# Folded query and key weights, a first group in halves, and a zero fill by DMA in a two-layer attention kernel

## The reference

```python
# first block
h = film(rmsnorm(x, norm1_w), cond, film1_w, film1_b)
Q = h @ q_w + q_b; K = h @ k_w + k_b; V = h @ v_w + v_b
attn = softmax(einsum('bnd,bmd->bnm', Q, K) * D ** (-0.5))
x = x + (einsum('bnm,bmd->bnd', attn, V) @ proj_w + proj_b)
h = film(rmsnorm(x, norm2_w), cond, film2_w, film2_b)
x = x + gelu(h @ mlp_w1 + mlp_b1) @ mlp_w2 + mlp_b2
# second block: mod = silu(c) @ ada_w.T + ada_b, in six parts
h = layernorm(x) * (1 + scale_msa) + shift_msa
x = x + gate_msa * attention(h, padding_mask)      # 16 heads of 8
h = layernorm(x) * (1 + scale_mlp) + shift_mlp
x = x + gate_mlp * (gelu_tanh(h @ fc1_w.T + fc1_b) @ fc2_w.T + fc2_b)
```

## Time and profile before

| | us |
|---|---|
| median of 3 runs | 182.25 |
| lowest and highest | 182.13, 182.42 |
| the profiled execution | 182.43 |
| its span, first to last instruction | 180.7 |
| busy: PE, PE weight load | 172.1, 133.9 |
| busy: DVE, ACT, POOL | 116.0, 107.7, 107.5 |

### The profile page before, as it was taken

The page is one execution under the profiler, slowest core; times in us unless marked ns, Lnnn a source line. Parts: engine busy times, 40 slices in busy tenths (PEclk is TensorE's granted clock), DMA queues, the critical chain, the costliest instruction groups (busy, mean ns, idle before and its releaser), DMA issues.

```text
span 180.7 us, 5691 instructions
## 1 busy us (share of the span) xinstructions
PE 172.1 (95%) x2250; PEld 133.9 (74%) x2250; DVE 116.0 (64%) x349; ACT 107.7 (60%) x274; POOL 107.5 (59%) x176
## 2 busy tenths in 40 slices
PE   6988999999999999989999999999899999999994
PEld 6965888587485798767678876888788765668594
DVE  0694569978106069867756878768688556696333
ACT  2338858871993651667576766767877596623500
POOL 5499979899910905995005333359979877690000
PEclk9999999999999999999999999999999999999999
DMA  4999999702247200300110001100000000001103
GB/s 111 341 425 429 424 421 426 337 13 39 51 175 308 102 0 4 120 7 3 62 39 32 2 5 64 64 2 5 5 7 7 5 0 5 0 0 58 62 0 116
DMA packets 5334, 19.31 MB, mean 107 GB/s; under 512 B 572, under 2 KB 1292, under 8 KB 3980
## 3 DMA queue, kind: packets, MB, share of 16 engines
q1 hardware_dynamic: 4988, 18.27, 26.2%
q10 hardware_dynamic: 320, 0.68, 1.2%
HBM read 7.24 MB, written 1.09 MB: 46 GB/s over the span
## 4 chain that ended last, share of the span: by engine, by line
PE 47%; POOL 26%; issue 17%; DVE 6%; DMA 3%; ACT 0%; POOLq 0%; ACTq 0%
PE ps L328 8%; PE ps L337 7%; PE ps L315 6%; PE ps L307 6%; PE ps L265 4%; POOL gtmp L1222 4%; POOL xb L1224 4%; POOL xc L1217 3%; POOL xn L1252 3%; POOL rstd L1143 3%; PE ps L239 3%; POOL xs L1231 3%; DMA xs<-x 3%; POOL gated L1228 3%; PE ps L270 2%
## 5 line engine op out<-in xcount | busy, mean ns | idle before, releaser
L1028 DVE TENSOR_REDUCE nm<-ps 128x4 f32<-128x512 f32 x64 | 42.1, 683 | 17.1 <-PE ps L380 16.6
L765 ACT ACTIVATE shared<-ps 128x512 f32<-128x512 f32 x64 | 34.5, 596 | 18.8 <-PE ps L380 18.8
L380 PEld LDWEIGHTS ps<-k_pad,q_pad 32*128 32x128 f32 x512 | 29.7, 186 | 9.7 <-issue 5.9
L380 PE MATMUL ps<-k_pad,q_pad 32*128 32x128 f32 x512 | 35.0, 282 | 1.7 <-DVE nm L1028 1.3
L380 PE MATMUL ps<-q_pad,k_pad 32*128 32x128 f32 x512 | 35.0, 283 | 0.0
L380 PEld LDWEIGHTS ps<-q_pad,k_pad 32*128 32x128 f32 x512 | 29.3, 186 | 0.4 <-issue 0.2
L1143 POOL TENSOR_TENSOR rstd<-var_eps,half 128x4 f32<-128x4 f32 x16 | 16.4, 1025 | 20.9 <-DVE var_eps L886 15.2
L1228 POOL TENSOR_TENSOR gated<-attn,gate 128x128 f32<-128x128 f32 x16 | 7.3, 459 | 27.2 <-ACT attn L784 27.2
L446 PE MATMUL ps<-shared,vx 128*32 128x128 f32 x512 | 17.3, 275 | 0.3
L813 ACT ACTIVATE hid<-ps,W 128x512 f32<-128x512 f32 x16 | 10.9, 688 | 9.7 <-PE ps L328 9.7
L446 PEld LDWEIGHTS ps<-shared,vx 128*32 128x32 f32 x512 | 13.1, 109 | 3.0 <-issue 1.5
(11 more groups left out here) (135 smaller groups left out, 330.6 us busy)
## 6 DMA issues: line engine op xcount, KB each, us to landing
q_pad<-hid SPq DMA_DIRECT2D x1, 4096.0 KB, 21.9
k_pad<-hid SPq DMA_DIRECT2D x1, 4096.0 KB, 30.9
gate<-gates SPq DMA_DIRECT2D x1, 2048.0 KB, 6.6
xs<-x SPq DMA_DIRECT2D x4, 256.0 KB, 6.6
gate<-mask SPq DMA_DIRECT2D x1, 1024.0 KB, 11.8
q_pad<-apT SPq DMA_DIRECT2D x4, 256.0 KB, 2.4
k_pad<-apT SPq DMA_DIRECT2D x4, 256.0 KB, 2.4
W<-weights SPq DMA_DIRECT2D x1, 768.0 KB, 9.9
```

The lines of the kernel that those rows point to most:

```text
L380: return mm(bank(to)[:, t], held[some, t, b], moved[some, t, b], start=True, stop=True, skip_group_check=True)
L765: a(pT[b % 2][:, r], bank(of), ACT.Exp, scale=HD ** -0.5).then_inc(s["c_exp"], 1)
L1028: v.tensor_reduce(nm[b % 2][:, 4 * r:4 * r + 4], bank(of), AX.X, ALU.max, negate=True).then_inc(s["c_max"], 1)
```

## The change

Scores are computed as h (s q_w k_w^T) h^T with s = 1/sqrt(128): the 128x128 matrix and three bias terms are computed once on the chip, by four products ahead of the first transposes, and copied by ACT with the scale. One product per group then gives the query side, and the normalised input itself is the key side. The bias term that depends on the row rides as column 129 of the value product, and the exponentials' bias is made from the negated maximum by two small DVE operations. ACT now copies the query, and copies the value in two instructions.

In group 0, statistics of tiles 0 and 1 are DVE's, of 2 and 3 ACT's (Square with a sum); POOL normalises tiles 0 and 2, DVE 1 and 3; transposes signal in halves, and DVE applies scale and shift to tiles 0 and 1 and ACT to 2 and 3; the query product runs in two halves. Of group 1, ACT normalises two of the four tiles. The rows (384 KB) go from ACT's queue to SP's, the first layer's attention weights (256 KB) from SP's to ACT's. The zeros come from the upper half of `gate` rather than from hid[1], and the two vx tiles are zeroed by two DMAs on SP behind those of q_pad and k_pad, under the same semaphore; POOL's memsets of vx go, and its ones are written later. The diff, cut to what matters:

```diff
-_W = [("cond", B), ("film1", 2 * C), ("film2", 2 * C), ("cols0", 16), ("q", C), ("k", C), ("vt", C),
+_W = [("cond", B), ("film1", 2 * C), ("film2", 2 * C), ("cols0", 16), ("qt", C), ("kt", C), ("vt", C),
...
+        flat = shared.rearrange("p a g n -> p (a g n)")
+        v0 = [flat[:, 1024 + 520 * u:1024 + 520 * u + 516].rearrange("p (g c) -> p g c", g=G) for u in range(2)]
+        folded = flat[:, 2064:2064 + 2 * C + 3]
+        wvp, key_row, key_mat, query_key, query_bias = (folded[:, a:b] for a, b in (
+            (0, C + 1), (C, C + 1), (C + 1, 2 * C + 1), (2 * C + 1, 2 * C + 2), (2 * C + 2, 2 * C + 3)))
...
@@ sync (SP)
             for g in range(2):
                 sp.dma_start(xs[:, G * g:G * g + G], x[:, G * g:G * g + G]).then_inc(s[f"x_in{g}"], 16)
-            for n, (a, b) in enumerate((("q", "x_end"), ("ada", "q1"), ("mlp1", "m_end"), ("q1", None))):
+            sp.dma_start(R[:, :], rows.partition_broadcast(128)).then_inc(s["rows_in"], 16)
+            for g in range(2, 4):
+                sp.dma_start(xs[:, G * g:G * g + G], x[:, G * g:G * g + G]).then_inc(s[f"x_in{g}"], 16)
+            for n, (a, b) in enumerate((("ada", "q1"), ("mlp1", "m_end"), ("q1", None))):
...
-            zeros = hid[1][:].rearrange("p f b n -> p (f b n)")
+            zeros = gate[:, B // 2:B].rearrange("n b g c -> n (b g c)")
             sp.wait_ge(s["zero_ok"], 1)
             for to in (q_pad, k_pad):
                 sp.dma_start(to[:].rearrange("p t b n -> p t (b n)"), zeros.unsqueeze(1).broadcast_to((128, 4, B * N)))\
                     .then_inc(s["pad_zero"], 16)
-            sp.wait_ge(s["pad_zero"], 32)
+            for to in vx:
+                sp.dma_start(to[:].rearrange("n b z -> n (b z)"), zeros).then_inc(s["pad_zero"], 16)
+
+            sp.wait_ge(s["pad_zero"], 64)
             sp.wait_ge(s["aug_ok"], 3)
...
@@ tensor (PE)
             def a_first_norm():
                 for j in range(G):
+                    pe.wait_ge(s[("a_xn", "a_xd")[j % 2]], j // 2 + 1)
                     ins = nc.tensor.transpose(bank(0 if j < 2 else 4)[:, j], xn[0][:, j], ident[:])
+                    if j % 2:
+                        ins.then_inc(s[("a_TA", "a_T")[j // 2]], 1)
+
+            def a_first_query():
+                pe.wait_ge(s["fold_ok"], 1)
+                for half in range(2):
+                    pe.wait_ge(s[("a_hd", "a_h")[half]], 1)
+                    ins = mm(ps[:, 1, 2 * N * half:2 * N * half + 2 * N], key_mat, hT[0][:, 2 * half:2 * half + 2],
+                             start=True, stop=True, skip_group_check=True)
+                ins.then_inc(s["a_Q"], 1)
...
-                mm(ps[:, 1 + n, :], w("qk"[n]), hT[g % 2][:], start=True, stop=True).then_inc(s[("a_Q", "a_K")[n]], 1)
+            def a_query(g):
+
+                pe.wait_ge(s["a_h"], g + 1)
+                pe.wait_ge(s["a_qT"], g)
+                mm(ps[:, 1, :], key_mat, hT[g % 2][:], start=True, stop=True).then_inc(s["a_Q"], 1)
...
                 for j in range(G):
-                    ins = mm(bank(3)[:, j], hT[g % 2][:, j], wvp[:], start=True, stop=True, skip_group_check=True)
+                    to = ps[:, 3, 129 * j:129 * j + 129] if j < 3 else ps[:, 2, 0:129]
+                    ins = mm(to, hT[g % 2][:, j], wvp, start=True, stop=True, skip_group_check=True)
...
-                    ins = mm(bank(4 + 3 * u)[:, j], qT[u][:, j], kT[u][:, j], start=True, stop=True, skip_group_check=True)
+                    ins = mm(bank(4 + 3 * u)[:, j], qT[u][:, j], hT[u][:, j], start=True, stop=True, skip_group_check=True)
...
             warm(6)
+            pe.wait_ge(s["w_attn0"], 16)
+            pe.wait_ge(s["qcol_ok"], 1)
+            at = 2 * N
+            for lhs, rhs, size in ((w("qt"), col("cols0", COL["k_b"]), 1), (w("qt"), w("kt"), C),
+                                   (w("kt"), col("cols0", COL["q_b"]), 1), (qcol[:], col("cols0", COL["k_b"]), 1)):
+                ins = mm(ps[:, 6, at:at + size], lhs, rhs, start=True, stop=True, skip_group_check=True)
+                at += size
+            ins.then_inc(s["fold_mm"], 1)
             a_first_norm()
...
+            a_first_query()
+            pe.wait_ge(s["a_xa"], 1)
+            a_norm(1)
             a_value(0)
-            a_norm(1)
             a_scores(0)
             for g in range(3):
-                a_qk(g + 1, 0)
-                a_qk(g + 1, 1)
+                a_query(g + 1)
                 a_value(g + 1)
...
@@ scalar (ACT)
-            act.dma_start(R[:, :], rows.partition_broadcast(128)).then_inc(s["rows_in"], 16)
+            act.dma_start(W[:, W_AT["qt"]:W_AT["x_end"]], weights[:, W_AT["qt"]:W_AT["x_end"]]).then_inc(s["w_attn0"], 16)
...
+            act.wait_ge(s["x_in0"], 16)
+            for j in range(2, G):
+                a(gtmp[:, j], xs[:, j], ACT.Square, accum_out=first_sum[:, j - 2:j - 1]).then_inc(s["a_sq0"], 1)
...
-            def a_kv(g):
-                act.wait_ge(s["a_K"], g + 1)
-                a(kT[g % 2][:], bank(2), ACT.Identity, bias=col("cols0", COL["k_b"])).then_inc(s["a_kT"], 1)
+            def a_q(g):
+                act.wait_ge(s["a_Q"], g + 1)
+                a(qT[g % 2], bank(1), ACT.Identity, bias=query_key).then_inc(s["a_qT"], 1)
+
+            def a_v(g):
                 act.wait_ge(s["a_V"], g + 1)
-                a(v0[g % 2][:], bank(3), ACT.Copy).then_inc(s["a_v"], 1)
+                a(v0[g % 2][:, 0:3], ps[:, 3, 0:387].rearrange("n (b c) -> n b c", b=3), ACT.Copy)
+                a(v0[g % 2][:, 3], ps[:, 2, 0:129], ACT.Copy).then_inc(s["a_v"], 1)
...
+            a(folded[:, C:2 * C + 3], ps[:, 6, 2 * N:3 * N + 3], ACT.Copy, scale=C ** -0.5).then_inc(s["fold_ok"], 1)
+            act.wait_ge(s["film_ok"], 1)
+            affine("a_", 0, 0, bank(4), range(2, G))
             act.wait_ge(s["wvp_mm"], 1)
...
+            for j in range(2, G):
+                ins = a(xn[1][:, j], xs[:, G + j], ACT.Copy, scale=rstd[:, 0, G + j:G + j + 1])
+            ins.then_inc(s["a_xa"], 1)
+            a_q(0)
             affine("a_", 1, 0, bank(0))
+            a_v(0)
             a_exp(0)
...
-            act.wait_ge(s["pad_zero"], 32)
             b_gelus(1, range(2))
...
@@ vector (DVE)
+            for j in range(2):
+                v.bn_stats(bn[:, j], xs[:, j]).then_inc(s["a_first"], 1)
...
             def a_max(g):
                 u = g % 2
                 dve.wait_ge(s["a_S"], g + 1)
                 v.tensor_reduce(amax[:, u, :], bank(4 + 3 * u), AX.X, ALU.max, negate=True).then_inc(s["a_max"], 1)
+                dve.wait_ge(s["a_max"], g + 1)
+                dve.wait_ge(s["a_v"], g + 1)
+                row_term = v0[u][:, :, C]
+                v.scalar_tensor_tensor(out=amax[:, u, :], in0=amax[:, u, :], scalar=query_bias, in1=row_term,
+                                       op0=ALU.subtract, op1=ALU.subtract).then_inc(s["a_true"], 1)
+                dve.wait_ge(s["a_true"], 2 * g + 1)
+                v.scalar_tensor_tensor(out=emax[:, u, :], in0=amax[:, u, :], scalar=query_bias, in1=row_term,
+                                       op0=ALU.add, op1=ALU.add).then_inc(s["a_true"], 1)
...
@@ gpsimd (POOL)
-            p.memset(hid[1][:].rearrange("p f b n -> p (f b n)"), 0.0).then_inc(s["zero_ok"], 1)
+            p.memset(gate[:, B // 2:B].rearrange("n b g c -> n (b g c)"), 0.0).then_inc(s["zero_ok"], 1)
...
+                if k == 0 and g == 0:
+                    pool.wait_ge(s["a_sq0"], 2)
+                    p.tensor_scalar(var_eps[:, 0, 2:G], first_sum[:], 1.0 / C, EPS, ALU.mult, ALU.add).then_inc(s["a_ms0"], 1)
...
+            p.tensor_scalar(qcol[:], ident[:], 0.0, col("cols0", COL["q_b"]), ALU.mult, ALU.add).then_inc(s["qcol_ok"], 1)
             p.tensor_scalar(bcol[:], ident[:], 0.0, col("cols0", COL["v_b"]), ALU.mult, ALU.add).then_inc(s["bcol_ok"], 1)
...
-            for u in range(2):
-                p.memset(vx[u][:].rearrange("n b z -> n (b z)"), 0.0).then_inc(s["c_vinit"], 1)
...
             norm(1, 3, "b_")
             next_bias(3)
+            pool.wait_ge(s["pad_zero"], 64)
+            for t in vx:
...
```

More of the change, by code:

```diff
@@ L82, in build @@
         arden = sb("arden", [N, 2, G])
-        wvp = sb("wvp", [C, C])
+        qcol = sb("qcol", [C, N])
+        emax = sb("emax", [N, 2, G])
         bias_a = sb("bias_a", [N, C])
@@ L161, in stats_end @@
             n = G * k + g
-            return PER_GROUP * (n if n else 1)
+            return PER_GROUP * (n - 1)
         K_BANK = (7, 6, 6, 6)
@@ L690, in a_exp @@
             def a_exp(g):
                 u = g % 2
[L692 removed]
+                act.wait_ge(s["a_true"], 2 * g + 2)
                 for j in range(G):
[L694 removed]
+                    a(p0[u][:, j], bank(4 + 3 * u)[:, j], ACT.Exp, bias=emax[:, u, j:j + 1],
                       accum_out=aden[:, u, j:j + 1]).then_inc(s["a_exp"], 1)
             act.wait_ge(s["x_in1"], 16)
+            act.wait_ge(s["a_sq0"], 2)
@@ L698, in _ @@
             for j in range(G):
```

(39 more changed lines are left out.)

92 lines of the change are left out of this document (38 added, 54 removed).

## The result

The changed kernel takes 186.0 us (median of 4 runs, 185.49 to 186.41), the kernel before 182.33 on the same chip: a ratio of 1.0183 (95% interval 1.0135 to 1.0231). The forecast was 184.5 with 183.2 to 187.0 around it. The direction held and the size was within the range, but the wait that I had named is not in the profile.

What follows compares the result with a forecast made beforehand. PE was taken as the bound. Fills delay the spreads to 63.9, PE arrives 1.2 us sooner at 60.4 and waits, +2.3 us: 182.43 + 2.3 - 0.2 = 184.5 us, range 183.2 to 187.0.

Steps and rivals of the forecast that it cites:

- the wait that I had named: Before whole_scores(0): PE arrives at 60.4 and stands 3.5 us for both spreads, to 63.9; end moves by +2.3 us.
- The bound: Whole kernel: PE is busy nearly throughout; whatever delays PE at one point delays the end by as much.
- The term that decided the sum: Second layer: two vx fills on SP's queue add 4.88 us, so spreads land at 63.9 behind the gate read; +2.3 us.
- the first exponential starts at 15.6, where it started before: First layer, group 0: ACT's value copy ends at 15.1, DVE's corrections wait for it, exponentials start unchanged at 15.6.
- PE enters the MLP 1.2 us sooner: End of first layer: the folding's saving, taken as 1.2 us between bounds of 0 and 3.4.
- two small dependent operations ... 0.6 us in all: First layer, DVE behind each maximum: two added operations, priced from one of 0.16 us plus similar waits, 0.6 us.
- Rival (c): First layer not shortened at all; same 184.5 while PE comes by 63.9, 2.3 us later; 0.62 together with the main case.
- likewise if PE's wait is elsewhere: Sign against the forecast: it is wrong if PE waits somewhere other than for a spread before the first L380 group.
- the main case: Fills delay the spreads, PE waits before whole_scores(0): 184.5 us, own range 183.8 to 185.2; 0.62 together with rival (c).
- Rival (a): Clock falls in PE's 3.5 us stand for the spreads, costing 2.4 us more: 186.9; chance 0.16.
- Rival (b): Spreads not held behind the gate read, so the front's gain is kept: 181.0; chance 0.16 whole, 0.03 partly.
- The signs named in advance: Aug_rows near 42.3, gate read near 56.3, spreads right behind, PE idle 3 to 4 us, MLP entered near 31.

Runs made afterwards that it cites:

- the maximum first: Changed kernel with DVE taking group 0's maximum and two corrections ahead of group 3's statistics, fills left in: 187.99 us (187.16 to 188.74).
- the old queues: Changed kernel with group 0's maximum ahead, vx zeroed by POOL, and rows and attention weights back on their previous queues: 183.38 us, ratio 0.9998.
- both edits: Changed kernel with group 0's maximum ahead of group 3's statistics and vx zeroed by POOL again: 183.21 us median of ten runs, ratio 1.0.

## Why the prediction was right, and where it was not

- **The bound** held: PE's time to whole_scores(0) went into the end whole. 2.88 us late there, 3.06 us in the profiled execution (185.49 against 182.43).
- **The term that decided the sum**, the fills, was right as a mechanism and a little small: SP was put back by 5.65 us, not 4.88, the landings behind took 1.89 and 0.44 us less than before, so that the gate read moved by only 3.1 us where I had 4.88; but with the spreads behind it, it took 8.3 us and not 6.6, and in the profile of the fills alone PE stood until 64.4, not 63.9. That the landing came so near the forecast is partly two errors of opposite sign. The fills alone give 185.8 against 182.3, 3.5 us with 2.3 forecast; the profiled run has 2.8, and the two runs that lie highest are those with a clock of 0.991.
- **The step that failed** is the first layer: "the first exponential starts at 15.6, where it started before", and from it "PE enters the MLP 1.2 us sooner". The exponential came at 19.63, and PE entered 2.88 later. Three profiles split this. With the maximum first and a quick start, PE enters at 30.53, 1.55 us sooner than before. The slow start costs 2.02 (32.55). DVE's order costs another 2.41 (34.96, with the same slow start). So 2.88 = 2.02 + 2.41 - 1.55.
- In DVE's part, two terms were wrong. That the statistics of group 3 stand ahead of the first maximum is not in the forecast, so it was put at nothing: the maximum started at 17.32 and not 16.18, 1.14 us. And "two small dependent operations ... 0.6 us in all" was priced by a row in which POOL was not in the way: in group 0 they took 1.56 us, since the first stood beside POOL's addition, 1.30 us instead of 0.22. Moving the maximum ahead takes away both (2.21 us at the first exponential). The start of PE, 12 warm products in 2.91 us or in 1.58, was not in the forecast at all; why it is slow in one execution and quick in another is open.
- Without the corrections the changed kernel (with vx by POOL, in a quick start) is 1.25 us ahead at whole_scores(0). That this is the 1.2 of the forecast is partly luck: the forecast had the corrections in it and nothing for the statistics, and with the corrections in place, the maximum first and a quick start the MLP starts 1.55 us ahead.
- **Rival (c)** is what the changed kernel's own profile shows: the front is late by itself. By my own sign, "likewise if PE's wait is elsewhere", the main case is refuted for this execution. I had said that (c) changes the stages and not the end as long as PE is at most 2.3 us late; it was 2.9, and the two delays hid each other. That is why 184.5 came near for half a wrong reason. In a quick start PE would come some 2 us sooner and then meet the spreads near 64.4, which gives about the same time if the clock does not fall there; this is an estimate from the profiles above, and no profile of the changed kernel has that start.
- **Rival (a)**, the clock, did not occur in the profile of the changed kernel, which has no stand there, but in the kernel with the maximum first, at 1.6 us where I had 2.4.
- **Rival (b)** is excluded: the spreads landed 6.6 us behind their issue when SP issued them behind the gate read, and after it.
- Two slips in the working move nothing: 42.87 shifted by 4.88 is 47.75, not 47.6, for the gates, and rival (b) takes the spreads' issue at 57.3 to 57.9 where the paragraph above it has 56.7 and 57.3.
- The signs named in advance did their work: the spreads' late issue at 60.12, the missing wait and the MLP entered at 35, not near 31, were what said that another cause was at work.

## What to carry over

Two delays that end at the same wait hide each other: taking one away may show little, or, if the clock falls in the stand that appears, even a loss; so undo each alone in the kernel before and both together in the changed one. Price a small operation on the way between a reduction and what waits for it by the slowest neighbour it can meet, not by its own length; here, an operation of 0.2 us took 1.3 in one group, and two of them 2.4 in another. Before a delay is laid to the edit, look for what differs between two executions of the same program; here, the start of PE alone moved the MLP by 2.0 us. Before hiding a fill in a DMA queue, follow what stands behind it in that queue to the last landing that an engine waits for.

## What was not expected of the hardware

- A small VectorE operation with two SBUF inputs lasted 1.30, 1.23 and 1.19 us when a GpSimd addition of 128x512 was running, 0.22 us otherwise.
- TensorE's granted clock fell to 1.2 GHz behind stands of 2.33, 2.44 and 2.84 us (from 19.9 to 23.3 in the first case, from 65.5 to about 68.9 in the last), and in the profile with the old queues behind two of 1.18 and 0.58 us (from about 31.4 to 34.8). It did not behind one of 3.12 us, nor in the changed kernel behind one of 2.28 us at the same place in the program as the one of 2.33. The length of the stand does not tell these apart.
- The mean granted clock of a run shows such falls without a trace: with both edits, the four runs between 181.6 and 182.0 have 1.00, the four between 183.1 and 183.4 have 0.991.
- At the start, the same 12 warm products took 1.58 us in some profiles and 2.91 in others, with the granted clock shown as 1.00 in both; with the same program in front, that was worth 2.0 us at the MLP. The kernel before has runs near 182.3 and some near 183.9, all with a clock of 1.00; that these are the two starts is not shown.
